# Gate logits and output projection of the last attention pass from one matmul of 273 columns, with the projected values copied out of PSUM by ScalarE

## The reference

```python
q_norm = q / jnp.linalg.norm(q, axis=-1, keepdims=True)
q_scaled = (q_norm + query_embedding[None]) * jax.nn.softplus(temperature)[None]
attn = softmax(einsum('bhqd,bhkd->bhqk', q_scaled, k) / sqrt(hd))
h = einsum('bhqk,bhkd->bhqd', attn, v)        # back to (tokens, 256)
gates = softmax(h @ Wr.T + br)                # 15 columns
mask = one_hot(top_k(gates, 3)).sum(-2)
routed_gates = gates * mask * 3
sw = softmax(h @ Ws.T + bs)                   # 2 columns
weight_0 = sw * 2
masked_gates = concat([weight_0[..., 0:1] * sw, weight_0[..., 1:2] * routed_gates])
out = (h * masked_gates.sum(-1, keepdims=True)) @ Wp.T + bp
```

## Time and profile before

| | us |
|---|---|
| median of 3 runs | 6720.48 (6718.82 to 6723.12) |
| the profiled execution's own time | 6723.68 |
| its span, first to last instruction | 6721.6 |
| TensorE busy in it | 5683.2 (85%) |
| VectorE | 5399.0 (80%) |
| ScalarE | 3825.4 (57%) |
| GpSimd | 2562.5 (38%) |

### The profile page before, as it was taken

The page is one execution under the profiler, slowest core; times in us unless marked ns, Lnnn a source line. Parts: engine busy times, 40 slices in busy tenths (PEclk is TensorE's granted clock), DMA queues, the critical chain, the costliest instruction groups (busy, mean ns, idle before and its releaser), DMA issues. The chain is left out here.

```text
span 6721.6 us, 142690 instructions
## 1 busy us (share of the span) xinstructions
PE 5683.2 (85%) x54804; PEld 3882.5 (58%) x54914; DVE 5399.0 (80%) x12498; ACT 3825.4 (57%) x7089; POOL 2562.5 (38%) x2572
## 2 busy tenths in 40 slices
PE   6999999687878878886899999999139888988988
PEld 4666666454545455553676677766126666666665
DVE  6878888588888888888787887888668888888887
ACT  5777777455555555553566666666325555555554
POOL 0122111122222222222354445444126666666665
PEclk9999999788888898987999999999569999999998
DMA  1111111100000000000011001100100000000000
GB/s 58 43 44 44 46 44 41 36 20 22 23 21 25 21 21 25 21 20 24 26 33 32 30 25 34 31 30 28 36 22 23 23 25 27 21 27 23 23 23 18
DMA packets 140390, 194.38 MB, mean 29 GB/s; under 512 B 25808, under 2 KB 63696, under 8 KB 139344
## 3 DMA queue, kind: packets, MB, share of 16 engines
q1 hardware_dynamic: 139728, 185.26, 8.7%
HBM read 113.03 MB, written 72.18 MB: 28 GB/s over the span
## 5 line engine op out<-in xcount | busy, mean ns | idle before, releaser
L1085 DVE TENSOR_REDUCE Amp<-pj 128x2 f32<-128x512 f32 x1024 | 644.6, 683 | 118.2 <-PE pj L800 118.2
L1085 DVE TENSOR_REDUCE Dmp<-pj 128x2 f32<-128x512 f32 x1024 | 641.1, 684 | 88.4 <-PE pj L800 86.4
L1085 DVE TENSOR_REDUCE Cmp<-pj 128x2 f32<-128x512 f32 x1024 | 642.8, 685 | 82.1 <-PE pj L800 80.9
L938 ACT ACTIVATE Dpr<-st 128x512 f32<-128x512 f32 x1024 | 529.2, 606 | 312.8 <-PE st L735 311.7
L938 ACT ACTIVATE Apr<-st 128x512 f32<-128x512 f32 x1024 | 528.6, 603 | 274.3 <-PE st L735 272.6
L938 ACT ACTIVATE Cpr<-st 128x512 f32<-128x512 f32 x1024 | 528.7, 603 | 174.6 <-PE st L735 172.6
L1020 POOL TENSOR_SCALAR Bve<-Bmv 128x2 f32<-128x2 f32 x128 | 29.1, 227 | 1339.4 <-DVE Bmv L1152 1339.4
L996 POOL TENSOR_TENSOR Dnrm<-Dnrm,power 128x32 f32<-128x32 f32 x64 | 348.8, 5449 | 196.5 <-DVE Dnrm L1063 196.5
L1020 POOL TENSOR_SCALAR Ave<-Amv 128x2 f32<-128x2 f32 x64 | 14.6, 228 | 1020.2 <-DVE Amv L1152 1020.2
L938 ACT ACTIVATE Bpr<-st 77x512 f32<-77x512 f32 x512 | 261.5, 592 | 191.7 <-PE st L735 191.0
L735 PE MATMUL st<-Aq,Ak 32*128 32x256 f32 x4096 | 330.4, 397 | 5.6 <-DVE Aq L1092 4.7
(11 more groups left out here) (310 smaller groups left out, 15553.9 us busy)
## 6 DMA issues: line engine op xcount, KB each, us to landing
Ax0T<-in_xT SPq DMA_DIRECT2D x64, 256.0 KB, 2.8
Ax<-in_x SPq DMA_DIRECT2D x64, 256.0 KB, 3.4
x_A_scratch<-Ax SPq DMA_DIRECT2D x64, 256.0 KB, 2.0
Bx<-x_A_scratch SPq DMA_DIRECT2D x64, 256.0 KB, 2.9
x_B_scratch<-Bx SPq DMA_DIRECT2D x64, 256.0 KB, 2.0
Cx<-x_B_scratch SPq DMA_DIRECT2D x64, 256.0 KB, 2.9
x_C_scratch<-Cx SPq DMA_DIRECT2D x64, 256.0 KB, 2.0
Dx<-x_C_scratch SPq DMA_DIRECT2D x64, 256.0 KB
```

Source lines behind the costliest of these rows:

```text
L938: ck.tell(act.activation(dst, st[bank][0:n, :], ACT.Exp, scale=HD ** -0.5), "probs_ready", step)
L1085: ins = dve.tensor_reduce(dst, src, AX.X, ALU.max, negate=True)
```

## The change

The output weights and the gate weights become one tile of 273 columns, `proj_gate`, filled by two DMAs ahead of pass D. At the gate's place TensorE does four matmuls of 273 columns, the two token tiles into two banks, which are told full one after the other. VectorE adds the bias to the 17 last columns of each bank in two operations. ScalarE copies the 256 first columns of each bank into `at` (SBUF), after VectorE has taken that bank's logits, and these copies free the banks; the exponentials follow them on ScalarE. At the place of `oproj` TensorE does nothing any more, and VectorE's scaled addition reads `at` instead of the bank. `gate` takes two banks and `oproj` of A4 none. `ORDER` stays as it is.

```diff
@@ bank_uses
+    if step[:2] == ("oproj", "A4"):
+        return []
-    if kind == "max":
+    if kind == "max" or kind == "gate":
         return [step + (0,), step + (1,)]
@@ signals
-        "gate": ["logits_taken", "dve_step", "logits_ready", "exps_ready"] + ["dve_step"] * 7,
+        "gate": ["proj_copied"] * 2 + ["logits_taken"] * 2 + ["dve_step", "logits_ready", "exps_ready"] + ["dve_step"] * 7,
@@ emptied_by
+    if kind == "gate":
+        return "proj_copied", use[:-1], use[-1]
@@ tiles
-        gate_w = sb("gate_w", [P, FC, H + 1])
+                self.proj_gate = sb("proj_gate", [P, FC, D + H + 1], F32, where) if phase == "D" else None
@@ TensorE
-                    elif kind == "oproj":
-                        if att != "A4":
-                            ck.wait("attnT_ready", ("oT", att, s))
+                    elif kind == "oproj" and att != "A4":
+                        ck.wait("attnT_ready", ("oT", att, s))
                         tokens(ck, step, w[f"{att}_wo"], atT[s], [(0, P), (P, P)])
                     elif kind == "gate":
                         ck.wait("attnT_ready", ("oT", att, s))
-                        ck.wait_bank_free(step)
                         for t in range(QT):
+                            ck.wait_bank_free(step + (t,))
                             for f in range(FC):
-                                ins = pe.matmul(ck.bank(step)[:, t * (H + 1):(t + 1) * (H + 1)],
-                                                atT[s][:, f, t * P:(t + 1) * P], gate_w[:, f, :],
-                                                start=(f == 0), stop=(f == FC - 1))
-                        ck.filled(ins, step)
+                                ins = pe.matmul(ck.bank(step + (t,))[:, 0:D + H + 1], atT[s][:, f, t * P:(t + 1) * P],
+                                                proj_gate[:, f, :], start=(f == 0), stop=(f == FC - 1))
+                            ck.filled(ins, step + (t,))
@@ ScalarE
                     elif kind == "gate":
+                        for t in range(QT):
+                            ck.wait_bank_full(step + (t,))
+                            ck.wait("logits_taken", step, nth=t)
+                            ck.tell(act.activation(at[s][:, t], ck.bank(step + (t,))[:, 0:D], ACT.Copy), "proj_copied", step)
                         ck.wait("logits_ready", step)
@@ VectorE
                     elif kind == "oproj":
-                        ck.wait_bank_full(step)
-                        bank = ck.bank(step)[:].rearrange("p (t d) -> p t d", t=QT)
                         ck.wait("base_ready", ("norm", att, s, 0))
                         if att == "A4":
+                            ck.wait("proj_copied", ("gate", att, s))
                             for t in range(QT):
-                                ins = dve.scalar_tensor_tensor(out=res[s][:, t], in0=bank[:, t], scalar=gs[s][:, 15, t:t + 1],
+                                ins = dve.scalar_tensor_tensor(out=res[s][:, t], in0=at[s][:, t], scalar=gs[s][:, 15, t:t + 1],
                                                                in1=res[s][:, t], op0=ALU.mult, op1=ALU.add)
...
                     elif kind == "gate":
-                        ck.wait_bank_full(step)
-                        src = ck.bank(step)[:, 0:QT * (H + 1)].rearrange("p (t n) -> p t n", t=QT)
-                        ins = (dve.tensor_tensor(lg[s][:], src, gate_b[:].unsqueeze(1).to_broadcast([P, QT, H + 1]),
-                                                 ALU.add))
-                        ck.tell(ins, "logits_taken", step)
+                        for t in range(QT):
+                            ck.wait_bank_full(step + (t,))
+                            ck.tell(dve.tensor_tensor(lg[s][:, t, :], ck.bank(step + (t,))[:, D:D + H + 1], gate_b[:], ALU.add),
+                                    "logits_taken", step)
                         ck.wait("logits_taken", step)
@@ SyncE, ahead of pass D
+                        if phase == "D":
+                            loads += [(tiles.proj_gate[:, :, 0:D], io["A4_wo"].rearrange("p (a b) -> p a b", a=FC)),
+                                      (tiles.proj_gate[:, :, D:D + H + 1], io["gate_w"].rearrange("p (a b) -> p a b", a=FC))]
```

More of the change, by code:

```diff
@@ L222, in bank_uses @@
     kind = step[0]
+    if step[:2] == ("oproj", "A4"):
+        return []
     if kind in ("q", "k", "v", "qT", "kT", "shift", "xT", "oT", "oproj", "xqT", "hT", "down",
-                "norm", "dist", "expand", "gate", "pv"):
+                "norm", "dist", "expand", "pv"):
         return [step]
-    if kind == "max":
+    if kind == "max" or kind == "gate":
         return [step + (0,), step + (1,)]
@@ L293, in emptied_name @@
             "hT": "hqT_ready", "down": "down_taken", "dist": "dist_ready", "expand": "x4_used",
-            "gate": "logits_taken"}[kind]
+            }[kind]
 SIGNALS = sorted({x for p in PASSES for step in entry(p, 0) for x in signals(step)})
@@ L396, in build @@
             loads = [(wf[0][:], io["w_gate"]), (wf[1][:], io["w_up"]), (wf[2][:], io["w_down"])]
[L397 to L398 removed]
+            loads += [(gate_b[:], io["gate_b"][None, :].partition_broadcast(P).rearrange("p o d -> p (o d)")),
                       (temp_sp[:], io["temperature"][None, :].partition_broadcast(P).rearrange("p o d -> p (o d)")),
@@ L482, in __init__ @@
                 att = PASSES[phase][0]
-                self.w = {n: sb(n, [P, FC, D], F32, where) for n in io["square_weights"] if n.startswith(att)}
+                self.w = {n: sb(n, [P, FC, D], F32, where) for n in io["square_weights"] if n.startswith(att) and n != "A4_wo"}
+                self.proj_gate = sb("proj_gate", [P, FC, D + H + 1], F32, where) if phase == "D" else None
                 self.row = {n: sb(n, [P, D], F32, where) for n in ALL_BIASES if n.startswith(att)}
@@ L550, in segment @@
             if phase == "D":
+                proj_gate = tiles.proj_gate
                 path, ctx, ends, sq, nrm = tiles.path, tiles.ctx, tiles.ends, tiles.sq, tiles.nrm
@@ L583, in bank @@
                 def bank(self, use):
-                    step = use[:-1] if use[0] in ("gu", "max") else use
+                    step = use[:-1] if use[0] in ("gu", "max", "gate") else use
                     return pj[counts.bank[self.latest[step], use][0]]
@@ L1109, in do @@
                     elif kind == "oproj":
-                        ck.wait_bank_full(step)
-                        bank = ck.bank(step)[:].rearrange("p (t d) -> p t d", t=QT)
                         ck.wait("base_ready", ("norm", att, s, 0))
                         if att == "A4":
+                            ck.wait("proj_copied", ("gate", att, s))
                             for t in range(QT):
-                                ins = dve.scalar_tensor_tensor(out=res[s][:, t], in0=bank[:, t], scalar=gs[s][:, 15, t:t + 1],
+                                ins = dve.scalar_tensor_tensor(out=res[s][:, t], in0=at[s][:, t], scalar=gs[s][:, 15, t:t + 1],
                                                                in1=res[s][:, t], op0=ALU.mult, op1=ALU.add)
                         else:
+                            ck.wait_bank_full(step)
+                            bank = ck.bank(step)[:].rearrange("p (t d) -> p t d", t=QT)
                             ins = dve.tensor_tensor(res[s][:], bank, res[s][:], ALU.add)
```

## The result

The changed kernel takes 6778.41 us (median of 4, 6772.78 to 6779.24); the kernel before, run again beside it, 6721.8 us (median of 4). The ratio is 1.008, with a 95% interval of 1.0066 to 1.0094: slower by 0.8%. The forecast of 6750 us had the direction right, and the result lies in its range, but the forecast gave +28 us to a step that grew by about twice that.

The account below looks back on a forecast made before the run. No single engine was taken to bound the last stage; the chain crosses TensorE and VectorE. Streams 0 + 0.25 + 1.0 + 0.5 = +1.75 us a turn, 16 turns, +28 us, plus 1.5 for the last sample: 6750 us (+0.44%), range 6714 to 6784.

Parts of the forecast that it names:

- What bounds the kernel: Last stage, turns of 105.5 us: TensorE 90% busy, VectorE 82%; work taken from one engine need not move the end.
- Stream 3, forecast 0: At stream 3's gate TensorE saves 0.94 us, but a path through GpSimd's power and VectorE takes it: 0 a turn.
- Stream 2, forecast +0.25: At stream 2's gate TensorE saves 0.91 us or more, but later second logits delay VectorE: +0.25 us a turn.
- Stream 1, forecast +1.0: Projection moves eleven steps earlier, so the norm's transposes, scaled addition and maxima come later: +1.0 us a turn.
- Stream 0, forecast +0.5: At stream 0's gate second logits come 1.0 us later, partly absorbed by L1217's wait on GpSimd: +0.5 us a turn.
- the clock falls on the chain: Rival, 25%: behind stream 0's gate the clock falls on the scores, 2.3 instead of 1.15 us; 6768 us.
- TensorE decides after all: Rival, 10%: paths beside TensorE at streams 3 and 2 have slack; -1.75 us a turn, 6694 us.
- partial gains: Rival, 18%: stream 3 gains none, stream 2 half of 0.91 us, stream 0's delay may vanish; 6728 us.
- Port: Scaled addition L1115, with two SBUF inputs, may be held up by GpSimd: priced at nothing, at most 0.4 us a turn.
- Copies, banks, DMA: ScalarE copies 0.4 us each, hidden in idle time; no bank change outside the stretch; loads 0 to 1 us once, left out.
- The long turns: Four longer turns' extra 14.6 us may vanish or double: +-15 us inside the range, no case of its own.

Follow-up runs that it names:

- the new form at 3 and 2: Against the kernel before, only streams 3 and 2 take the changed form, streams 1 and 0 keep separate gate and projection: 6720.03 us, ratio 0.9995.
- the short power: Kernel before with GpSimd's power replaced by a product of constants, leaving out the query norm: 6699.39 us; with streams 3 and 2 changed too: 6665.64 us.
- stream 0 filled: The changed kernel plus unread matmuls only at the old place of stream 0's projection: 6772.5 us, ratio 1.0063 to the kernel before.
- not merged: Against the changed kernel, projection still moved to the gate's place, but gate logits are separate matmuls ahead of it; one ScalarE copy: 6758.93 us, ratio 1.0051.
- the unread matmuls at 47 us: Changed form at streams 3 and 2 only, plus two unread matmuls in TensorE's wait between stream 1's first two maxima: 6716.5 us, ratio 0.9982.

## Why the prediction was right in its direction and short in its size

- **What bounds the kernel: right.** No engine alone does. TensorE lost 1.6 us of work a turn and the turn grew by 3.7.
- **Stream 3, forecast 0: right in size,** +0.02 us measured, **and its reason right in part.** The chain goes through GpSimd's power and normalization (5538.33, 5.46 us) and not through the gate. But with the power gone only 0.22 of the 0.94 us comes through: ScalarE's exponentials hold TensorE's next scores, a wait that the forecast hadn't named.
- **Stream 2, forecast +0.25: wrong in sign by 0.6 us.** Measured -0.35, and -0.37 in a regular turn of the kernel with the new form at 3 and 2. The term had two sides, and I let the later second logits win. The matmuls behind this gate ran at half clock before and run at full clock now (8 in 1.89 us at 5566.05). The clock isn't what the gain rests on, though. Between turns without any fall, with the short power, the same stretch (stream 0's `v` to stream 1's gate) still shrinks by 0.31 us, from 42.65 to 42.34. Of the 2.3 us that TensorE is spared there, 0.35 arrive, and of the 0.91 without the clock 0.31.
- **Stream 1, forecast +1.0: right, a little high.** +0.72 measured in the table by places, +1.02 as a mean with the new form at stream 1 alone. In that second figure the hole ahead of stream 0's gate is included, so the two agree less well than they seem.
- **Stream 0, forecast +0.5: the step that failed,** +3.33 measured. Two things in it were wrong, and both are shown. The lateness of the second logits, for which the 0.5 stood, costs 0: in the kernel with the new form at stream 0 alone the scores start at +10.29, against +10.39 before. VectorE took the old logits only at 5491.62, behind its own statistics, so they came 0.5 later and not 1.0, and the stretched operations behind them (L1217 of 0.58 us) ran in 0.19 and gave that back. And the clock, which I set apart as a rival at 25%, is the whole of what was lost.
- **The rival "the clock falls on the chain" was the right mechanism with half its price.** Its text priced the scores at +1.15 us a turn for 6768 us; they measure +0.94. It missed the other half, 1.97 us ahead of the scores. I asked what the removal of stream 0's projection leaves on TensorE, and did not ask the same of stream 1's, which I priced only by what comes later. Its removal turns a wait of 0.80 us into one of 1.58 us, 2.4 us before stream 0's gate, and the clock then falls on the gate. That wait could be worked out from before: the projection's eight matmuls stood there.
- **TensorE decides after all, partial gains: fell.** The changed kernel is 84 and 50 us above them. The second one's sum had a slip: 1.05 less stream 0's 0.5 is 0.55 us a turn and not 0.4, so 6731 and not 6728.
- **Port: right at nothing.** L1120 takes 478 ns in the middle and 536 at most, against 476 and 485. As far as the trace's spans go, 62 of the 128 additions overlap a GpSimd operation that reads SBUF: the 32 beside the power alone take 474 to 478 ns, the 30 at its small successors 479 to 536, the 66 beside none 473 to 485. The Trainium skill (SBUF — State Buffer, Who interferes with whom) has an operation with two SBUF inputs contend with GpSimd's reads, the later one blocked in full. These 62 don't show it: the longest was held for some 60 ns, beside operations of up to 5.46 us.
- **Copies, banks, DMA: right.** 0.38 us for 256 columns, inside idle time of ScalarE. No new wait for a bank was found on the chain; the loads cost 0.3 us.
- **The long turns** shrank from 14.6 to 109.69 x 15 - 109.23 x 15 = 6.9 us, inside the +-15.
- **That the result lies in the range is in part luck.** The regular turn was to be 107.3 us and is 109.23. The other three streams were forecast at +1.25 together and measure +0.39, and the long turns gave 7.7 us back; without these 7.7 the time would be 6786, above the range's 6784. That upper end came from a rival that had half of the mechanism.

What stays open: why the clock falls at one of two turns with the same waits and starts, as with the new form at stream 0 alone, and where the next fall comes when one is removed. The rows show the fall and the wait ahead of it, and not what the chip counts. The Trainium skill (TensorE: Matmul & The Clock Gate, the section on HAM oscillation) names gaps in a stream of matmuls as what throttles it. The falls here agree in that they follow waits, but the waits are shorter: its example has waits for DMA of about 3 to 5 us, here 0.8 to 1.6 us between stretches of dense work were enough. It also says that this can come back at each such gap, and the 16 of 16 turns agree.

## What to carry to other kernels

Before work is taken from TensorE, read the waits on both sides of the place it leaves, of every place: work off the chain can be what keeps the clock up for work on it. Here useless matmuls in the old places won back 30 us. In this kernel the merged form cost nothing, and won nothing measurable, where dense matmuls follow the gate (streams 3 and 2), and cost time where the next matmuls wait for small operations of another engine (streams 1 and 0). Compare single turns with the same falls and not only means: that gives the price without the clock. And a fall that is removed can come back later in the turn, so look at the turn and not only at the place.

## What the hardware showed that was not expected

- A wait of 0.80 us ahead of stream 0's gate left it at full clock in 16 of 16 turns of the kernel before, and in 15 of 16 with the new form there alone. A wait of 1.58 us at the same place left none of 16 wholly at full clock, in each of four kernels (the change, stream 0 filled, new form at stream 1 alone, not merged). In the change this costs 1.97 us for 0.78 us of idle time.
- Eight matmul instructions of 17 columns take 1.04 us and are followed by the lower clock at stream 2 in the kernel before; eight of 273 take 2.10 there in the changed kernel and are not.
- Removing one fall moved another: the unread matmuls at 47 us gave a fall at 68 us, and the turn kept its length. So did filling stream 0's place alone, which gave falls at 49 to 50 or 70 us.
